# Batch 1's projections and all of its row maxima moved into batch 0's attention, and a second load queue for the first score operands

## What is computed

```python
q = jnp.concatenate([q1, q2], axis=1); k2 = jnp.repeat(k, 2, axis=1); v2 = jnp.repeat(v, 2, axis=1)
scores = jnp.where(causal, jnp.einsum('bhqd,bhkd->bhqk', q, k2) * scale, jnp.finfo(scores.dtype).min)
y = jnp.einsum('bhqk,bhkd->bhqd', softmax(scores), v2)
y1, y2 = (y[:, :H], y[:, H:])
y = y1 - sigmoid(x @ Wlam) * y2
x = layernorm(x + y @ Wo)
x = layernorm(x + shared_mlp(x) + routed_mlp(x) * comb_w)
```

## Time and profile before

| what | value |
|---|---|
| median of 3 runs | 481.25 us (480.75 to 482.18) |
| the profiled execution | 481.01 us, its span 479.3 us |
| busy PE, PEld | 88%, 70% of the span |
| busy DVE, POOL, ACT | 59%, 51%, 50% |
| chain that ended last | PE 71%, DVE 13%, ACT 5% |
| HBM read, written | 27.94 MB, 11.53 MB |

### The profile page before, as it was taken

How to read it: one execution, slowest core, us unless ns; L and a number is a source line. 1 busy time by engine, 2 the same in 40 slices (tenths; PEclk the granted TensorE clock), 3 DMA queues, 4 the chain that set the end, 5 groups by cost and what they waited for, 6 DMA issues and landing times.

```text
span 479.3 us, 10336 instructions
## 1 busy us (share of the span) xinstructions
PE 419.5 (88%) x4008; PEld 334.3 (70%) x4008; DVE 282.3 (59%) x676; ACT 237.9 (50%) x532; POOL 244.4 (51%) x334
## 2 busy tenths in 40 slices
PE   5139697899998999999999999999999999898995
PEld 4126146765997679875987679865987679765895
DVE  3627137853758376754757375745757477837374
ACT  4704472477254843476254843475355841384240
POOL 8305374557254934567354835566364831393142
PEclk9759699999999999999999999999999999999999
DMA  8762760363023610371124511380024410000000
GB/s 295 227 149 70 203 171 1 112 166 69 1 71 100 154 45 21 102 179 35 35 78 113 132 45 27 98 199 25 23 82 109 113 45 1 4 1 24 1 22 24
DMA packets 34753, 40.41 MB, mean 84 GB/s; under 512 B 4240, under 2 KB 28304, under 8 KB 34448
## 3 DMA queue, kind: packets, MB, share of 16 engines
q1 hardware_dynamic: 34704, 39.75, 30.5%
HBM read 27.94 MB, written 11.53 MB: 82 GB/s over the span
## 4 chain that ended last, share of the span: by engine, by line
PE 71%; DVE 13%; ACT 5%; issue 3%; DMA 3%; SPq 2%; POOL 2%; POOLq 0%; DVEq 0%; ACTq 0%
PE ff L665 10%; PE ff L667 9%; PE ff L666 9%; PE ybank L777 8%; DVE neg_max L1009 7%; PE ring L749 6%; PE ring L728 5%; PE ybank L665 4%; PE ring L753 3%; PE ybank L666 3%; PE ybank L667 3%; PE ybank L790 3%; PE ring L723 3%; ACT prob L512 2%; DVE xz L1115 2%
## 5 line engine op out<-in xcount | busy, mean ns | idle before, releaser
L1009 DVE TENSOR_REDUCE neg_max<-ring 128x2 f32<-128x512 f32 (+3 forms) x176 | 104.4, 637 | 45.9 <-PE ring L728 45.2
L512 ACT ACTIVATE prob<-ring 128x512 f32<-128x512 f32 x192 | 100.9, 613 | 15.9 <-PE ring L749 15.8
L397 POOL TENSOR_TENSOR h_lo<-h_full,h_hi 128x256 fp32r<-128x256 f32 x72 | 52.9, 735 | 97.7 <-ACT h_hi L472 97.7
L407 POOL TENSOR_SCALAR_AFFINE_SELECT prob<-prob 128x512 f32<-128x512 f32 x128 | 83.8, 678 | 27.2 <-ACT prob L512 27.0
L665 PE MATMUL ff<-x1T_hi,wg_lo 128*128 128x256 f32 x288 | 85.7, 297 | 0.1
L666 PE MATMUL ff<-x1T_lo,wg_hi 128*128 128x256 f32 x288 | 80.2, 278 | 0.0
L667 PE MATMUL ff<-x1T_hi,wg_hi 128*128 128x256 f32 x288 | 80.1, 278 | 0.0
L520 ACT ACTIVATE gate_t<-ff 128x256 f32<-128x256 f32 x72 | 27.6, 384 | 75.0 <-PE ff L667 72.2
L1030 DVE COPY yv<-ybank 128x256 f32<-128x256 f32 x64 | 27.1, 423 | 63.5 <-PE ybank L777 63.1
L723 PE MATMUL ring<-mask_b,ident_b 128*128 128x128 bf16 (+2 forms) x176 | 44.6, 253 | 19.7 <-DMA q_stack<-qk_parts_dram 17.6
L728 PE MATMUL ring<-k_stack,q_stack 96*128 96x256 bf16 (+3 forms) x512 | 58.9, 235 | 0.0
(11 more groups left out here) (164 smaller groups left out, 885.5 us busy)
## 6 DMA issues: line engine op xcount, KB each, us to landing
q_stack<-qk_parts_dram SPq DMA_DIRECT2D x48, 256.0 KB, 4.5
qk_parts_dram<-parts SPq DMA_DIRECT2D x72, 128.0 KB
k_stack<-qk_parts_dram SPq DMA_DIRECT2D x48, 128.0 KB, 4.4
xt_raw<-xT SPq DMA_DIRECT2D x8, 256.0 KB, 2.8
xz<-x SPq DMA_DIRECT2D x8, 256.0 KB, 2.8
out<-xz SPq DMA_DIRECT2D x7, 256.0 KB, 2.2
prob<-w_gu SPq DMA_DIRECT2D x1, 1152.0 KB, 7.5
yv<-w_gu SPq DMA_DIRECT2D x1, 1024.0 KB, 9.9
```

The source lines that it names most:

```text
L397: pool.tensor_tensor(h_lo[:, n, :], h_full[:, n % RING, :], h_hi[:, n, :].bitcast(F32), ALU.subtract).then_inc(h_lo_done, 1)
L407: pool.affine_select(out=v, in_=v, compare_op=ALU.is_ge, fill=0.0, base=0, pattern=[[0, 2], [HALF, 2], [0, 2], [1, HALF]], channel_multipl ...
L512: act.activation(prob[:, g % RING, u, :], ring[u][:, :], ACT.Exp, scale=SCALE).then_inc(exp_done, 1)
L1009: dve.tensor_reduce(neg_max[:, columns.start:columns.stop, i], ring[u % RING][:, 0:len(columns) * keys].rearrange("p (h k) -> p h k", k=keys),
```

## The change

- Stack 0: ACT issues the 6 loads of part 0 right after `values(0, t)`, and SP issues the 6 of parts 1 and 2 after its stores (`load_part`). The load of batch 1's transposed input goes ahead of the nine stores on SP, and its split on ACT ahead of the other weight splits. SP waits for all of stack 0 before it stores parts of batch 1.
- Batch 1's three projections stand before `first_scores(0)` on PE, and no longer between score units.
- SP writes batch 0's maxima after the 12 loads of stack 1, no longer before them.
- Batch 1's 22 score units, in the two `ff` banks, stand in the second pass of batch 0: two after each `t_group` (from group 0 on), and four in the last step, each before the value product of that step. DVE makes their maxima there, ahead of the step's evacuation.
- `max_job(1)` stands right after `wo_job(0)`. `max_first(1)` is the first thing in ACT's iteration 1, ahead of `split_xt(2)`; `load_max(1)` follows `load_x(1)` on SP.
- Iteration 1 on PE is then: the three projections of batch 2, the transposes of batch 0's rows, router, logits, gate/up units 0 to 3, second pass.

```diff
+        def load_part(queue, b, p):
+            queue.wait_ge(parts_stored[p], (b + 1) * (16 * QK_JOBS))
...
+        def s_bank(b, u):
+            return ff[u % 2] if b == EARLY else ring[u % RING]
+        def early_units(step):
+            last = GROUPS + 1
+            return range(step * EARLY_STEP, S_UNITS if step == last else (step + 1) * EARLY_STEP)
             def iteration(i, has_next=True, has_last=True):
                 load_x(i)
+                if i == EARLY:
+                    load_max(i)
+                if is_first(i):
+                    sp.wait_ge(stack_loaded, 16 * STACK_LOADS)
                 if has_next:
                     store_parts(i + 1, range(QK_JOBS))
                 if i + 2 < B:
                     load_xt(i + 2)
-                load_max(i)
+                if i not in (0, EARLY):
+                    load_max(i)
                 if has_next:
-                    load_stacks(i + 1)
+                    load_stacks(i + 1, range(3))
+                if is_first(i):
+                    load_max(i)
...
+            load_xt(1)
             for n, p in ((0, 0), (1, 0), (0, 1), (2, 0), (1, 1), (2, 1), (0, 2), (1, 2), (2, 2)):
                 store_part(0, n, p)
-            load_xt(1)
-            load_stacks(0)
+            load_stacks(0, range(1, 3))
...
             def iteration(i, has_next, has_prev, has_last):
+                if i == EARLY:
+                    max_first(i)
                 if has_next:
-                    split_xt(i + 1)
+                    if has_prev:
+                        split_xt(i + 1)
                     raw_part(i + 1, 0)
...
             for t in range(TT):
                 values(0, t)
+            load_part(act, 0, 0)
+            split_xt(1)
             split_weight(wo_hi[:, :, :], wo_raw, wo_loaded)
...
             def s_unit(b, u):
-                if u == 0:
+                if b == EARLY:
+                    if u > 1:
+                        pe.wait_ge(max_done, b * S_UNITS + u - 1)
+                elif u == 0:
...
                 if not has_prev:
+                    for n in range(QK_JOBS):
+                        qk_job(i + 1, n)
                     first_scores(i)
-                for u in range(S_UNITS):
+                if i == EARLY:
+                    for n in range(QK_JOBS):
+                        qk_job(i + 1, n)
+                    x1T_job(i - 1)
+                    router_job(i - 1)
+                    logit_job(i - 1)
+                for u in range(S_UNITS if i != EARLY else 0):
...
                     if g < GROUPS:
                         t_group(i, g)
+                    if i + 1 == EARLY:
+                        if g == 0:
+                            first_scores(i + 1)
+                        for u in early_units(g):
+                            if u > 0:
+                                s_unit(i + 1, u)
                     if g >= 2:
                         pv_group(i, g - 2, has_next)
...
                 wo_job(i)
+                if i + 1 == EARLY:
+                    max_job(i + 1, False)
...
                 for g in range(GROUPS):
+                    if i + 1 == EARLY:
+                        for u in early_units(g + 2):
+                            row_max(i + 1, u)
...
                     evacuate_pv(i, g)
```

More of the change, by code:

```diff
@@ L81 @@
 PROJ_CHUNKS = QK_JOBS + 1
+EARLY = 1
+EARLY_STEP = 2
 W_PROJ = PROJ_CHUNKS
@@ L241, in qk_bank @@
             return (ybank[0], ybank[1], misc if is_first(b) else ybank[0])[n]
+        def load_part(queue, b, p):
+            queue.wait_ge(parts_stored[p], (b + 1) * (16 * QK_JOBS))
+            for s in range(SLOTS):
+                rows = slice(s, STACK_ROWS, SLOTS)
+                if Q_PARTS[s] == p:
+                    queue.dma_start(q_stacks[b % STACKS][rows, :, :, :], scratch[p, :, :, 0:Q_JOBS, :]).then_inc(stack_loaded, 16)
+                if K_PARTS[s] == p:
+                    queue.dma_start(k_stacks[b % STACKS][rows, :, :, :].rearrange("p r h t -> p r (h t)"), scratch[p, :, :, Q_JOBS, :]).then_inc(stack_loaded, 16)
+        def s_bank(b, u):
[3 more added lines that the diff above has]
+            return range(step * EARLY_STEP, S_UNITS if step == last else (step + 1) * EARLY_STEP)
         block = ctx.enter_context(nc.Block())
@@ L261, in store_parts, with load_stacks @@
                         store_part(b, n, p)
-            def load_stacks(b):
+            def load_stacks(b, parts):
                 if b >= STACKS:
                     sp.wait_ge(t_full, (b - STACKS + 1) * T_UNITS)
[L266 to L274, removed]
+                for p in parts:
+                    load_part(sp, b, p)
             def load_max(b):
@@ L599, in iteration @@
                     mlp_units(i - 1, (FF_FIRST,))
-                max_first(i)
+                if i != EARLY:
+                    max_first(i)
                 if has_prev:
@@ L719, in s_unit @@
                     pe.wait_ge(max_done, b * S_UNITS + u - RING + 1)
-                bank = ring[u % RING]
+                bank = s_bank(b, u)
                 i, columns, keys = s_job(u)
@@ L742, in t_group @@
                 for u in range(3):
-                    if g == 0:
+                    if g == 0 and b == EARLY:
+                        if u == 0:
+                            pe.wait_ge(exp_done, b * T_UNITS - RING + 1)
+                        else:
+                            pe.wait_ge(v_done, b * TT + u)
+                    elif g == 0:
                         pe.wait_ge(max_done, b * S_UNITS + S_UNITS - RING + u + 1)
@@ L816, in x1T_job @@
                 pe.wait_ge(yT_lo_done, b + 1)
+                if b + 1 == EARLY:
+                    pe.wait_ge(max_l_done, EARLY + 1)
                 for t in range(TT):
@@ L919, in iteration @@
                     gu_units(i - 1, (FF_FIRST,))
-                max_job(i, has_prev)
+                if i != EARLY:
+                    max_job(i, has_prev)
                 if has_prev:
@@ L1008, in row_max @@
                 i, columns, keys = s_job(u)
-                dve.tensor_reduce(neg_max[:, columns.start:columns.stop, i], ring[u % RING][:, 0:len(columns) * keys].rearrange("p (h k) -> p h k", k=keys),
+                dve.tensor_reduce(neg_max[:, columns.start:columns.stop, i], s_bank(b, u)[:, 0:len(columns) * keys].rearrange("p (h k) -> p h k", k=keys),
                                   AX_X, ALU.max,
@@ L1144, in iteration @@
                     norm_mean(0, *before)
[L1145 to L1149, removed]
+                if i == EARLY:
+                    max_second(i)
+                    x1T_second(i - 1)
+                    router_top(i - 1, router_steps[0])
+                else:
+                    for u in range(1, S_UNITS):
+                        row_max(i, u)
+                        if has_prev and u - 2 == X1T_AT:
                             x1T_second(i - 1)
-                        if u - 1 == LOGIT_AT:
+                        if has_prev and u - 1 == LOGIT_AT:
                             router_top(i - 1, router_steps[0])
@@ L1161, in iteration @@
                             router_sum(i - 1, *router_steps)
+                if i + 1 == EARLY:
+                    for step in range(2):
+                        for u in early_units(step):
+                            row_max(i + 1, u)
                 for g in range(GROUPS):
+                    if i + 1 == EARLY:
+                        for u in early_units(g + 2):
+                            row_max(i + 1, u)
                     if g == 0 and is_first(i):
@@ L1179, in iteration @@
                 yT_second(i)
-                if i + 1 < B:
+                if i + 1 < B and i + 1 != EARLY:
                     row_max(i + 1, 0)
```

8 lines of the change are left out of this document (5 added, 3 removed).

## The result

The changed kernel takes 488.53 us (median of 4 runs, 488.09 to 491.27), the kernel before 481.72 beside it (480.75 to 482.67): ratio 1.0144, interval 1.0121 to 1.0168. It is slower, as forecast, by 6.8 us instead of 3.5, and the time lies 0.5 us outside the range given (480.0 to 488.0). The profiled execution took 488.98 us with a span of 487.3.

What follows compares the result with a forecast made beforehand. PE was taken as the full engine, busy 88% of the span, left without work by two transfers. -2.2 + 5.6 - 1.0 + 1.1 = +3.5 us on 481.01 gave 484.5 us, range 480.0 to 488.0.

Steps and rivals of the forecast that it cites:

- The second pass: Batch 0's second pass: 22 added score units, less gaps and cold time, plus waits for maxima, cost +5.6 us.
- The normalisation: After batch 0's second pass: POOL's splits end earlier against DVE's work, -1.0 us, ends -2.2 and 0.
- Iteration 1: Batch 0's output product to batch 1's second pass: -0.7 us warm, 1.8 charged for half clock, +1.1 us.
- the start: Kernel start to batch 0's second pass: stack 1 and the maxima land earlier, 50.8 instead of 52.97, -2.2 us.
- its last term: Stack 1's loading before batch 0's second pass: 13.4 us from first load issue at 37.1 to landing at 50.5.
- 10.5 us: Chain of ACT and POOL from batch 1's `raw_part` to the last third part, 10.5 us as before, ending at 36.0.
- Stack 0 lands near 29: In the start: with issue from 16.1 instead of 18.35, stack 0 lands near 29, buying nothing by itself.
- From there on ... a shift is handed on unchanged: After iterations 0 and 1: every wait is as before, so any shift is handed on unchanged.
- The clock did not stay up: Rival in iteration 1: projections and transposes may suffice to keep the clock up, 482.7 us; chance 0.17.
- the slots hid little: Rival at ACT's six issues and second-pass gaps: cheap issues, half the units hidden, 477.8 us; chance 0.13.
- stack 1 came later and not sooner: Rival at the start: stack 1 comes sooner, batch 0's second pass starts at 49, 481.7 us; chance 0.10.
- "slower start" rival: At the start: competing loads, ACT's issues at 1.3 us each, stack 1 near 54, cold stretch 8.3 us, 488.5 us; chance 0.10.

Runs made afterwards that it cites:

- units twice: The kernel before with 22 further score units, each with its maximum, in batch 0's second pass, batch 1's units still in iteration 1: 485.58 us.
- filler units: The changed kernel with 21 score units of batch 1 made once more in iteration 1, unused and without maxima: 485.63 us.
- the run with one queue: The changed kernel with all 12 loads of stack 0 on SP again, ACT issuing none: 489.29 us.
- the start alone: The changed kernel with batch 1's score units back in iteration 1 and batch 0's maxima written before stack 1 is loaded: 476.88 us, ratio to before 0.9882.

## Why the prediction was right or wrong

**The sign and most terms held.** The second pass was forecast 5.6 us longer and is 5.6 (22.2 against 16.6): PE full, the last units waiting for maxima. The exact hit is luck, though. The half clock was to last 6.7 us and lasted 4.6, which gives 1.9 back and not 0.8; units, gaps and waits together cost 7.5 and not 6.4 (6.3 - 0.9 + 1.0). The two errors of 1.1 cancel; units twice shows the same 7.5. The normalisation was to give 1.0 back, with 2.2 as the end, and gives 1.9; both DVE waits are gone and not one and a bit. That the rule on the shared access of VectorE and GpSimd (the Trainium skill, SBUF — State Buffer, Who interferes with whom) was the right reading is borne out: the trace after has the same operations at 0.17 and 0.43 us with POOL out of the way. Iteration 1 was forecast 1.1 us longer in spite of 6.3 us less work, and is 1.3; the wait for `xt_lo`, the idle PE and the half clock are all in the rows, and filler units show that the clock is the larger part (2.3 us, priced at 1.8; the rest was priced at -0.7 and is -1.0).

**The step that failed is the start.** The prediction had "-2.2 us" and it is +0.9. Its chain was the right one, from ACT's `raw_part` over the stores to stack 1 with the maxima behind it, and its last term held (40.23 to 53.88 is 13.65 us, 13.4 taken). Two terms of it were missing. ACT was to issue from 16.1, when its values are done; it waited until 17.76, for the third store of part 0 had not landed. The working gave that wait nothing, though the diff has it in `load_part`. And POOL's first rest was priced within "10.5 us" taken from a time when DVE was idle; now it falls on DVE's weight splits and takes 2.59 us instead of 1.16. 1.7 + 1.4 is 3.1, and stack 1's first load is issued at 40.23 instead of 37.1. Taking ACT's loads away moved the whole chain, `raw_part` from 27.19 to 21.00 and POOL's last part from 39.1 to 32.9, and with the second chain out of the way too the start fell to 50.36. The six issues at 0.65 each were priced well.

"Stack 0 lands near 29" failed too (31.8): 13.0 us had been counted from 16.1, while the first load went out at 17.76. That explains 1.7 of the 2.7 us; the rest may be input x, loaded from 23.28 on, which no run separates. It did no harm in the changed kernel by itself, as the prediction said, but the run with one queue shows it as a second bound just behind the first: SP's nine stores wait for it.

**"From there on ... a shift is handed on unchanged"** was wrong by up to 2 us: 377.4 became 379.5 in the profiles, 1.6 of it in the last iteration with its low clock. 0.9 + 3.7 + 1.3 + 2.1 is the 8.0 us between the two spans; the medians are 6.8 apart, so 1.2 of the 8.0 are particular to the two profiled executions, and which term holds them isn't shown. So the forecast's 3.5 misses the profile's 8.0 by 3.1 at the start and 2.1 behind iteration 1, less 0.7 in between.

**The rivals.** The clock did not stay up, the slots hid little, stack 1 came later and not sooner. The "slower start" rival had 488.5 us. It put the late stack 1 on issues at 1.3 us each and added a cold stretch of 8.3 us; the place was right, the cause another and the cold stretch 4.6, so its number is luck too. I gave it 0.10. What I did not see is the comparison that matters: the start alone, with the maxima ahead of stack 1, gains 4.7 us, and the changed kernel gives it up so that units can be made where PE is full.

## What to carry to other kernels

Move work to a stage only where the engine that does it has room, and look at what else the move makes urgent: here a transfer that had 13 us of slack became the one the pass waits for. Work on an engine that isn't the bound may still be what keeps its clock up; taking it out made the kernel before slower and putting useless copies into the changed kernel made that one faster, so the gain of removing it must be tested and not summed. When a chain is shortened without effect, look for a second one that ends at the same wait.

## What the runs showed of the hardware

- PE's granted clock fell to half in iteration 1 (0.50 from 96 on), after PE had worked 0.24 us of the 2 us before, and adding 21 units without use kept it at 1.00. It also fell while PE was fairly busy, in the first pass of batch 0 in the kernel after: 1.59 us of 2 worked, and half clock from 38 on.

```profile
36.00:38.00 2.00, 1.59 (x12) 0.69 (x12) 2.00 (x6) 0.63 (x1) 1.20 (x3) 0.99 0.44 125
38.00:41.30 3.30, 3.25 (x20) 1.91 (x21) 3.30 (x7) 0.00 (x0) 1.08 (x1) 0.50 0.49 139
```

- POOL and DVE took turns: POOL's rest, 1.16 us alone, ran from 28.39 to 30.98 across the end of DVE's split (29.96), and DVE's next split, 0.42 us before the change, took 1.38 and ended behind POOL's. The delays, 1.4 us for POOL and 1.0 for DVE, are about what the other had left when they began (1.6 and 1.1).
- ACT issues a load in 0.65 us, as SP does, and while both issued, SP's loads of the q stack took 6.9 to 9.1 us to land instead of 4.0 to 6.8; the median of ACT's own three was 4.3.
